# A small FFN computed on two token halves in half-width TensorE tiles

## The reference, cut to what matters

```
x = x + 0.5 * ffn(layernorm(x))
x = x + attn(layernorm(x))          # delta-rule attention, then a 512-2048-512 MLP
x = x + 0.5 * ffn(layernorm(x))

def ffn(x):                         # M = 64 units, INNER = 16 hidden values per unit
    s = einsum('btd,dm->btm', x, Win) + bin_
    h = relu(s[..., None] * W1 + b1)                 # (tokens, 64, 16)
    g = einsum('btmh,mh->btm', h, W2) + b2           # each unit's 16 values summed
    return einsum('btm,md->btd', g, Wout) + bout
```

## Time and profile before

| | |
|---|---|
| median of 3 runs | 3695.51 us (3686.24 to 3698.28) |
| the profiled execution | 3692.6 us, its span 3690.6 us |
| TensorE's mean granted clock | 0.962 of full speed |
| busy: PE, PEld | 3364.3 us (91%), 2637.4 us (71%) |
| busy: DVE, ACT, POOL | 1886.2 us (51%), 1327.8 us (36%), 1147.5 us (31%) |
| stage 1 / stage 2 / stage 3 | about 0 to 1215, 1215 to 2000, 2000 to 3691 us |

### The profile page before, as it was taken

One profiled execution on the slowest core, in us unless ns is written; L12 is line 12 of the kernel. 1 busy time (PEld: TensorE's weight loads), 2 busy tenths in 40 slices (PEclk: granted clock), 3 DMA queues, 4 the chain that ended last, 5 costly groups with the idle time before them and its releaser, 6 DMA issues. The chain is left out here.

```text
span 3690.6 us, 150931 instructions
## 1 busy us (share of the span) xinstructions
PE 3364.3 (91%) x68430; PEld 2637.4 (71%) x68430; DVE 1886.2 (51%) x3292; ACT 1327.8 (36%) x2630; POOL 1147.5 (31%) x1207
## 2 busy tenths in 40 slices
PE   3988888888896899999997899999999999999997
PEld 2666666666665688888886677777777777777775
DVE  4767766667664887877832233332333333333323
ACT  4434333344331233333333333333333333333332
POOL 0334435354452655555520112221121122122211
PEclk7999999999998899999998999999999999999998
DMA  3244353444334666665655110001000111000000
GB/s 90 81 150 121 105 159 115 115 137 133 110 122 143 196 193 192 200 192 182 187 173 167 65 35 24 23 35 35 24 35 35 35 35 35 35 30 17 35 35 23
DMA packets 388102, 355.46 MB, mean 96 GB/s; under 512 B 58128, under 2 KB 320912, under 8 KB 384912
## 3 DMA queue, kind: packets, MB, share of 16 engines
q1 hardware_dynamic: 385632, 351.27, 30.4%
q10 hardware_dynamic: 2224, 0.90, 0.1%
HBM read 184.19 MB, written 153.09 MB: 91 GB/s over the span
## 5 line engine op out<-in xcount | busy, mean ns | idle before, releaser
L1784 DVE TENSOR_TENSOR glo<-gl,gh 128x512 fp32r<-128x512 f32 x256 | 195.1, 762 | 927.3 <-ACT gh L1691 927.2
L1687 ACT ACTIVATE gl<-bank,b1m 128x512 f32<-128x512 f32 x256 | 175.9, 687 | 796.4 <-PE bank L231 796.4
L229 PE MATMUL bank<-w_hi,gh 128*128 128x512 f32 x1024 | 410.6, 401 | 24.3 <-DVE glo L1784 24.3
L229 PE MATMUL bank<-h_hi,w_hi 128*128 128x512 f32 x1024 | 425.9, 416 | 4.0 <-DVE w_lo L1828 4.0
L231 PE MATMUL bank<-w_hi,glo 128*128 128x512 f32 x1024 | 406.7, 397 | 0.0
L230 PE MATMUL bank<-h_lo,w_hi 128*128 128x512 f32 x1024 | 406.4, 397 | 0.0
L231 PE MATMUL bank<-h_hi,w_lo 128*128 128x512 f32 x1024 | 406.3, 397 | 0.0
L230 PE MATMUL bank<-w_lo,gh 128*128 128x512 f32 x1024 | 405.5, 396 | 0.0
L398 PE MATMUL bank<-qk,rawk 32*32 32x64 f32 x8192 | 166.4, 230 | 117.9 <-DVE pb L767 110.6
L398 PEld LDWEIGHTS bank<-qk,rawk 32*32 32x32 f32 x8192 | 138.4, 114 | 172.2 <-issue 170.6
L970 POOL TENSOR_TENSOR nrm<-nrm,cst 128x16 f32<-128x16 f32 x64 | 185.6, 2900 | 198.1 <-DVE nrm L738 197.8
(11 more groups left out here) (172 smaller groups left out, 7214.8 us busy)
## 6 DMA issues: line engine op xcount, KB each, us to landing
ringB<-heads_scratch SPq DMA_DIRECT2D x256, 192.0 KB, 2.7
ringA<-heads_scratch SPq DMA_DIRECT2D x258, 128.0 KB, 2.2
X<-in_L_attn_x SPq DMA_DIRECT2D x16, 1024.0 KB, 9.7
x_scratch<-X SPq DMA_DIRECT2D x16, 1024.0 KB, 5.5
heads_scratch<-vb SPq DMA_DIRECT2D x16, 1024.0 KB, 11.3
heads_scratch<-qk SPq DMA_DIRECT2D x16, 1024.0 KB, 11.0
heads_scratch<-kb SPq DMA_DIRECT2D x16, 1024.0 KB, 5.2
heads_scratch<-kbuf SPq DMA_DIRECT2D x16, 1024.0 KB, 7.7
```

The costliest lines, as they stand in the source:

```text
L229: e.matmul(o, lhs[0], rhs[0], start=first, stop=False)
L1687: e.activation(gl[k][:, :], bank[k][:, :], ACT.Gelu_apprx_tanh, bias=b1m[:, m:m + 1]).then_inc(a_gl, 1)
L1784: e.tensor_tensor(gh[k][1][:, :], gl[k][:, :], gh[k][0][:, :], ALU.subtract).then_inc(v_gl, 1)
```

## The change

The 128 partitions of the FFN's arrays hold 64 units and two halves of the inner values before; after it they hold 64 units and two halves of the tile's tokens. All 16 inner values of a unit are gathered on one partition, for 256 tokens.

- `hidden`: eight products instead of four, each of 128 rows, 64 weight columns and 256 moving columns; token half k writes partitions 64k to 64k+63 of the bank's first 256 columns, in tile position k of the array.
- `relus` and `sums`: 16 instructions of 128x256 instead of 8 of 128x512 in each; four buffers of half the size, so an activation waits for the sum four before it. Their places in the order of ACT and DVE stay, with two instructions where one was.
- `ffn_out`: four products of 64 rows instead of 128, with the blocks in the order 0, 2, 1, 3, so that neighbours use different rows of the array and different banks.
- At the start `b2t` is loaded on both halves (one DMA more, 16 instead of 15), and POOL's memset of it and the wait on that are gone; the tables `w1t`, `b1t`, `w2t` are 128x16.

The diff, cut (stage 3 is changed in the same way as stage 1):

```diff
+HALF = TOK // 2
+INNER = 16
+FFN_ORDER = (0, 2, 1, 3)
...
+    def units(pairs):
+        return [2 * q + k for q in pairs for k in range(2)]
...
-            relu1 = [sbuf(st, f"relu{i}", [P, TOK]) for i in range(2)]
-            g1 = sbuf(st, "g1", [P, TOK])
+            relu1 = sbuf(st, "relu", [P, 4, HALF])
+            g1 = sbuf(st, "g1", [P, HALF])
...
                 for f in range(NF):
-                    m = e.matmul(bank[WIN_BANK][:, :], win[:, f, :], xT1[:, f, :], start=f == 0, stop=f == NF - 1)
+                    for k in range(2):
+                        r = slice(64 * k, 64 * k + 64)
+                        m = e.matmul(bank[WIN_BANK][r, 0:HALF], win[:, f, r], xT1[:, f, k * HALF:(k + 1) * HALF],
+                                     start=f == 0, stop=f == NF - 1)
                 m.then_inc(p_win, 1)
-                released[WIN_BANK] = a_relu, 8 * t + 8
+                released[WIN_BANK] = a_relu, INNER * t + INNER
 
             def ffn_out(t):
-                e.wait_ge(v_g, 8 * t + 8)
-                for b in range(NB):
-                    bk = 6 + b % 2
+                e.wait_ge(v_g, INNER * t + INNER)
+                for n, b in enumerate(FFN_ORDER):
+                    bk, k = 6 + n % 2, b // 2
+                    r = slice(64 * k, 64 * k + 64)
                     bank_free(bk)
-                    e.matmul(bank[bk][:, :], g1[:, b * P:(b + 1) * P], wout[:, :],
+                    e.matmul(bank[bk][:, :], g1[r, b % 2 * P:(b % 2 + 1) * P], wout[r, :],
                              start=True, stop=True).then_inc(p_wout, 1)
-                    released[bk] = v_x1, 4 * t + b + 1
+                    released[bk] = v_x1, 4 * t + n + 1
...
             def relus(t, *hs):
-                for h in hs:
+                for h in units(hs):
...
-                    if 8 * t + h >= 2:
-                        e.wait_ge(v_g, 8 * t + h - 1)
-                    e.activation(relu1[h % 2][:, :], bank[WIN_BANK][:, :], ACT.Relu, bias=b1t[:, h:h + 1],
+                    if INNER * t + h >= 4:
+                        e.wait_ge(v_g, INNER * t + h - 3)
+                    e.activation(relu1[:, h % 4, :], bank[WIN_BANK][:, 0:HALF], ACT.Relu, bias=b1t[:, h:h + 1],
                                  scale=w1t[:, h:h + 1]).then_inc(a_relu, 1)
...
-            loads.append((b2t[0:64, :], col(a["L0_ffn_b2"])))
-            e.wait_ge(o_zb2, 1)
...
             def sums(t, *hs):
-                for h in hs:
-                    e.wait_ge(a_relu, 8 * t + h + 1)
+                for h in units(hs):
+                    e.wait_ge(a_relu, INNER * t + h + 1)
...
-                        e.wait_ge(v_g, 8 * t + h)
-                        e.scalar_tensor_tensor(g1[:, :], relu1[h % 2][:, :], w2t[:, h:h + 1], g1[:, :],
+                        e.wait_ge(v_g, INNER * t + h)
+                        e.scalar_tensor_tensor(g1[:, :], relu1[:, h % 4, :], w2t[:, h:h + 1], g1[:, :],
                                                ALU.mult, ALU.add).then_inc(v_g, 1)
 
             def add_ffn(t):
-                for b in range(NB):
-                    e.wait_ge(p_wout, 4 * t + b + 1)
+                for n, b in enumerate(FFN_ORDER):
+                    e.wait_ge(p_wout, 4 * t + n + 1)
                     e.wait_ge(v_xb, 4 * t + b + 1)
-                    e.tensor_tensor(X[t % 2][:, b, :], bank[6 + b % 2][:, :], X[t % 2][:, b, :],
+                    e.tensor_tensor(X[t % 2][:, b, :], bank[6 + n % 2][:, :], X[t % 2][:, b, :],
                                     ALU.add).then_inc(v_x1, 1)
...
-            e.memset(b2t[:, :], 0.0).then_inc(o_zb2, 1)
```

More of the change, by code:

```diff
@@ L129, in macaron @@
         wout = sbuf(top, "wout", [P, D])
-        w1t = sbuf(top, "w1t", [P, 8])
-        b1t = sbuf(top, "b1t", [P, 8])
-        w2t = sbuf(top, "w2t", [P, 8])
+        w1t = sbuf(top, "w1t", [P, INNER])
+        b1t = sbuf(top, "b1t", [P, INNER])
+        w2t = sbuf(top, "w2t", [P, INNER])
         bint = sbuf(top, "bint", [P, 1])
@@ L1497, in macaron @@
             ss3 = sbuf(st, "ss3", [P, NB])
-            relu3 = [sbuf(st, f"relu3{i}", [P, TOK]) for i in range(2)]
+            relu3 = sbuf(st, "relu3", [P, 4, HALF])
         stage3 = [xT3[:, f, :] for f in range(NF)] + [Z[1][:, b, :] for b in range(NB)]
@@ L1588, in hidden, with ffn_out @@
                 for f in range(NF):
-                    m = e.matmul(bank[6][:, :], win[:, f, :], xT3[:, f, :], start=f == 0, stop=f == NF - 1)
+                    for k in range(2):
+                        r = slice(64 * k, 64 * k + 64)
+                        m = e.matmul(bank[6][r, 0:HALF], win[:, f, r], xT3[:, f, k * HALF:(k + 1) * HALF],
+                                     start=f == 0, stop=f == NF - 1)
                 m.then_inc(p_win, 1)
-                released[6] = a_relu3, 8 * t + 8
-            def ffn_out(t, b):
-                bk = 6 + b % 2
-                if b == 0:
-                    e.wait_ge(v_g3, 8 * t + 8)
+                released[6] = a_relu3, INNER * t + INNER
+            def ffn_out(t, n):
+                b = FFN_ORDER[n]
+                bk, k = 6 + n % 2, b // 2
+                r = slice(64 * k, 64 * k + 64)
+                if n == 0:
+                    e.wait_ge(v_g3, INNER * t + INNER)
                 bank_free(bk)
-                e.matmul(bank[bk][:, :], g3[:, b * P:(b + 1) * P], wout[:, :],
+                e.matmul(bank[bk][:, :], g3[r, b % 2 * P:(b % 2 + 1) * P], wout[r, :],
                          start=True, stop=True).then_inc(p_wout, 1)
-                released[bk] = v_o, 4 * t + b + 1
+                released[bk] = v_o, 4 * t + n + 1
             def up(t, m):
@@ L1711, in relus @@
             def relus(t, *hs):
-                for h in hs:
+                for h in units(hs):
                     if h == 0:
                         e.wait_ge(p_win, NT + t + 1)
-                    if 8 * t + h >= 2:
-                        e.wait_ge(v_g3, 8 * t + h - 1)
-                    e.activation(relu3[h % 2][:, :], bank[6][:, :], ACT.Relu, bias=b1t[:, h:h + 1],
+                    if INNER * t + h >= 4:
+                        e.wait_ge(v_g3, INNER * t + h - 3)
+                    e.activation(relu3[:, h % 4, :], bank[6][:, 0:HALF], ACT.Relu, bias=b1t[:, h:h + 1],
                                  scale=w1t[:, h:h + 1]).then_inc(a_relu3, 1)
@@ L1808, in sums @@
             def sums(t, *hs):
-                for h in hs:
-                    e.wait_ge(a_relu3, 8 * t + h + 1)
+                for h in units(hs):
+                    e.wait_ge(a_relu3, INNER * t + h + 1)
                     if h == 0:
@@ L1813, in sums, with add_ffn @@
                             e.wait_ge(p_wout, 4 * (NT + t))
-                        e.tensor_scalar(g3[:, :], relu3[0][:, :], w2t[:, 0:1], b2t[:, 0:1],
+                        e.tensor_scalar(g3[:, :], relu3[:, 0, :], w2t[:, 0:1], b2t[:, 0:1],
                                         ALU.mult, ALU.add).then_inc(v_g3, 1)
                     else:
-                        e.wait_ge(v_g3, 8 * t + h)
-                        e.scalar_tensor_tensor(g3[:, :], relu3[h % 2][:, :], w2t[:, h:h + 1], g3[:, :],
+                        e.wait_ge(v_g3, INNER * t + h)
+                        e.scalar_tensor_tensor(g3[:, :], relu3[:, h % 4, :], w2t[:, h:h + 1], g3[:, :],
                                                ALU.mult, ALU.add).then_inc(v_g3, 1)
-            def add_ffn(t, b):
-                e.wait_ge(p_wout, 4 * (NT + t) + b + 1)
+            def add_ffn(t, n):
+                b = FFN_ORDER[n]
+                e.wait_ge(p_wout, 4 * (NT + t) + n + 1)
                 e.wait_ge(o_xb3, 4 * t + b + 1)
-                e.tensor_tensor(Z[t % 2][:, b, :], bank[6 + b % 2][:, :], Z[t % 2][:, b, :], ALU.add).then_inc(v_o, 1)
+                e.tensor_tensor(Z[t % 2][:, b, :], bank[6 + n % 2][:, :], Z[t % 2][:, b, :], ALU.add).then_inc(v_o, 1)
             def split(i):
```

12 lines of the change are left out of this document (6 added, 6 removed).

## The result

The changed kernel takes 3738.02 us (median of 4 runs, 3722.89 to 3744.1) where the kernel before took 3696.9 us beside it (3686.24 to 3702.12): the ratio is 1.0103, 95% interval 1.0083 to 1.0124. It is slower by 1.0%; the prediction was 3730 us, 0.9%. The profiled execution has a span of 3720.9 us, 30.3 more than before, and a mean granted clock of 0.949 (0.962 before). It is the fastest of the four; the medians lie 41 us apart, and the traces show where 30 of them are.

What follows compares the result with a forecast made beforehand. PE sets the pace but waits for DVE's sums in both stages. Stage 3 +9, stage 1 +17, clock +8 and start +0.6 make +35 us: 3730 us, 0.9% slower; own range 3710 to 3755, 8 in 10 from 3693 to 3772.

Steps and rivals of the forecast that it cites:

- `hidden`: On PE, two column tiles at nearly two times speed make `hidden` about 1.5 us shorter (between 0 and 1.7).
- a pair of `ffn_out`: On PE, each pair of output products gets 0.75 us shorter (between 0 and 0.85).
- a turn beside POOL: Stage 3: DVE and POOL alternate instruction by instruction, so a half-sum beside POOL takes a turn of 1.44 us.
- stall in front of `down(7)`: Stage 3, PE waiting for `gelu_low(7)`: the stall grows from 0.6 to about 2.7 us a tile.
- stage 3, a tile: Later sums against shorter `ffn_out` pairs: net +0.6 us a tile, +9 us for 15 tiles (bounds -5 and +22).
- stage 1, DVE from `bs` to the end of the long stall: Stage 1, per tile: six sums ahead of the mask +2.0 us, meetings with POOL +0.5, ReLU wait gone -1.0.
- The last tile: The FFN running alone at the end: hidden -1.5, first ReLU -0.2, eight sums +2.7, output products about -1.0: 0 us.
- The clock: Stage 1: longer stalls in front of `gram(t-1, 6)` lower PE's clock behind more of them: +8 us (0 to +12).
- Cancelled: Rival, chance 0.16: full overlap, small additions don't add, clock falls no more often: about 3698 us, within 11 of before.
- the gain arrives: Rival, chance 0.10: DVE doesn't alternate with POOL, its short sums go through in a row; stage 3 gains -57: 3665 us.
- No overlap in `hidden`: Rival, chance 0.12: the two tiles share array rows, so sixteen passes take at least 3.45 us: 3758, up to 3785.
- The clock falls in stage 3 too: Rival, chance 0.12: stalls of 2.7 and 1.5 us lower PE's clock in stage 3, 2.3 us a tile: 3765 us.

Runs made afterwards that it cites:

- split_sums: Kernel before with only ReLUs and sums split into 16 instructions of 128x256, PE's products unchanged: 3773.9 us, ratio 1.0205.
- both edits: In stage 1 DVE's masks ahead of later sums, and POOL's add_x1 after the previous tile's sums: 3639.23 us on the changed kernel, 3639.43 on the one before.
- out_twice: Changed kernel with both edits, each product of stage 1's `ffn_out` issued twice: 3636.17 us, ratio 0.9825.
- split_out: Changed kernel with both edits, stage 1's `ffn_out` in two halves with a projection between, `add_ffn` halved too: 3604.09 us, ratio 0.9734.
- late_pool: Changed kernel with POOL's add_x1 in stage 3 waiting for the sums of the tile before: 3669.32 us, ratio 0.9925.
- half_units: Changed kernel with 8 of the 16 inner values of each unit left out in both stages, PE's FFN products unchanged: 3626.57 us, ratio 0.9807.
- both_before: Kernel before the change with both edits: 3639.43 us, ratio 0.9836.
- late_pool_before: Kernel before the change with POOL's add_x1 in stage 3 waiting for the sums of the tile before: 3679.58 us, ratio 0.9944.

## Why the prediction was right

The forecast's mechanism held: the doubled sums reach PE in both stages, at POOL's additions in stage 3 and ahead of the mask in stage 1. That the total came within a few us is luck in part, since several terms were off and cancel. One by one:

| term | predicted | measured |
|---|---|---|
| spacing of half-sums alone (last tile) | 0.60 us | (8.73 - 0.49) / 14 = 0.59 |
| half-ReLU | 0.57 us | 0.565 |
| DVE busy in all | +60 us | +63.3 |
| `hidden` | -1.5 us (1.9 to 2.0 left) | -1.65 (1.95) |
| a pair of `ffn_out` | -0.75 us | 1.13 in place of 1.98, but the passes behind it only 0.65 and 0.46 sooner |
| a turn beside POOL | 1.44 us | 1.432 |
| stall in front of `down(7)` | 2.7 us | 2.30 |
| stall in front of `ffn_out`, stage 3 | near 1.5 us | 1.44 |
| `ffn_out` of stage 3 starts later by | 2.2 us | 1.52 |
| stage 3, a tile | +0.6 us | +0.60 in 11 of 14 |
| stage 1, DVE from `bs` to the end of the long stall | 2.0 + 0.5 - 1.0 = +1.5 us a tile | +1.0 |
| stage 1, wait for ReLUs | -1.0 us a tile | 22.9 to 6.5 us in all |
| stage 1, second pair of `ffn_out` | -0.3 us | -0.33 in 9 tiles |
| first tile starts | +0.6 us | +0.2 |
| the end | 0 | +0.1 |

**Stage 3.** The period of a tile, from one stall in front of `down(7)` to the next, was 101.31 us on average and is 101.91 in 11 of 14 tiles, +0.60 as forecast, but by two misses that cancel. Counted from the start of `hidden`, `gelu_low(7)` ends after 12.8 us (12.6 before; I had 13.2) and `ffn_out` starts after 17.36 (15.84 before; I had 18.0), so PE loses 1.5 us there and not 2.2. The two pairs give back 1.0 of it and not 1.5: by its rows a pair is 0.85 us shorter, but a row's duration has the pipeline's end in it. From the start of the first pair to the second pass behind it there are 1.40 us where there were 2.05, and 1.40 where there were 1.95 at the second pair, which itself starts 0.09 us later behind the pass before it; another 0.1 is lost ahead of the next `hidden`.

**The last tile** was a sum of four numbers that should cancel, and did. DVE there, without POOL:

```profile
3700.57 0.41 DVE L1829 TENSOR_SCALAR g<-relu,w2t,b2t 128x256 f32<-128x256 f32 x1 [10.04 <-ACT relu L1732]
3701.09 8.73 DVE L1833 SCALAR_TENSOR_TENSOR g<-relu,w2t,g 128x256 f32<-128x256 f32 x15
```

**Stage 1**: from the end of one tile's `turn_h` wait to the end of the long stall a tile takes 1.28 us more on average over 14 tiles (1.54 without the last one); without the clock I had 2.0 + 0.5 - 1.0 = 1.5. Over 14 tiles that is +18. But not all of it is DVE's. From `bs` on it is 1.0 us; the other 0.55 lies ahead of `bs`, where DVE waits for PE's first projections, and PE goes from `turn_h` to `hidden` at a granted clock of 0.888 instead of 0.922. split_sums shows the doubled sums' part by itself, +1.8 from `bs` on, without what the shorter `hidden` gives back.

**The clock** is where the prediction was wrong in place. I put +8 us behind the long stall, also because 2.90 us of stall had left the clock alone; the trace has a second stall of 2.90 us, which ends at 153.34, and there it fell to 0.50 from 155 to 157. Behind the long stall nothing was added: from its end to the third product of `ffn_out` there are 11.6 us in both kernels, though the stall grew by 2.3. (With both edits, where the stall grows from 2.8 to 4.2 us, the same stretch does grow, from 10.80 to 11.72 us: there the mechanism that I had in mind shows.) Instead the clock falls at `ffn_out`, in 5 of the 14 tiles, whose stretch from the third product on takes 27.9 to 29.0 us where all took 26.75 before and the other nine now take 26.4. That is 5 x 1.7 = +8.5 us, so near to my 8 by chance; the 0.55 us a tile ahead of `bs`, some 7 us in all, I had not counted. The cause at `ffn_out` is the idle time that my own gain made: shorter products end sooner, DVE frees the bank no earlier, and 1.09 us of idle time become 1.75. I had counted the gain that "goes into that stall" as nothing; it was worse than nothing. out_twice and split_out show it from two sides.

**The rivals.** *Cancelled* and *the gain arrives* fell with +30 us in the span. The second's mechanism doesn't happen, since DVE does alternate with POOL, and its condition, DVE undisturbed, was made by late_pool. The rule of the Trainium skill (SBUF — State Buffer, SBUF: two separate sides) bears on the turns: between a DVE instruction with two SBUF inputs, as these sums are, and a GpSimd instruction that reads SBUF, whichever starts first holds the shared pair of ports for its whole instruction and the other waits. The steps of 1.432 us agree with it. *No overlap in `hidden`* fell with 1.95 us. The rule behind it (the Trainium skill, TensorE: Matmul & The Clock Gate, Part 3, The mechanism: a weight load overlaps with matmuls in flight only when its row group differs) would have kept sixteen passes on the same rows apart; the measurement decides against reading it so here, at 1.95 us side by side and 2.86 in turn, both below the 3.60 of eight passes on the full array. Weight loads of the full array run beside passes as well: in the trace before, one of 0.19 us starts at 2293.16, 0.01 us behind a pass of 0.40.

*The clock falls in stage 3 too* (chance 0.12) was half right. It does fall, behind the stall in front of `down(7)` in 8 tiles and behind `ffn_out` in one. In the tile whose `hidden` starts at 3213.35, PE and then its clock:

```profile
3226.21 0.79 PE L238 MATMUL bank<-w_hi,gh 128*128 128x512 f32 x1 [2.32 <-DVE glo L1799]
...
3227.65 0.63 PE L238 MATMUL bank<-w_hi,gh 128*128 128x512 f32 x1
...
3230.73 1.13 PE L1613 MATMUL bank<-wout,g 64*128 64x512 f32 x4
```

```profile
3226.00:3230.00 4.00, 3.79 (x10) 3.03 (x11) 3.37 (x8) 3.46 (x7) 0.00 (x0) 0.57 0.00 0
3230.00:3234.00 4.00, 4.00 (x18) 2.36 (x17) 2.46 (x5) 0.15 (x1) 0.00 (x0) 1.00 0.00 0
```

The passes take 0.63 instead of 0.40 us, but what stands behind them is the same end of the sums: the stall of 1.44 us in front of `ffn_out` is gone, `ffn_out` starts 4.52 us behind `down(7)` as in the tile without a fall, and the tile is as long as its neighbours (101.88 us). Where the clock fell behind `ffn_out` (0.57 from 2516 to 2520), nothing covered it: that tile took 104.13 us. I had priced each fall at 2.3 us without asking what stands behind it; the price is right only where PE has no wait left. Two more tiles took 102.53, one with a fallen clock and one without; in these three DVE waits 0.46 us for a ReLU amid its last sums, and `ffn_out` starts 4.87 us behind `down(7)`. What the three take over 101.91 is 3.5 us together. With 14 x 0.60 that is 11.9; stage 3 rose by 10.7, since the stretch ahead of its first `hidden` is 1.6 us shorter.

Expectations of the experiments were wrong too. half_units gained 7.4 us in stage 1 where 38 were expected: the stretch that ends with the mask gave 1.8 us a tile instead of 2.5 to 3, and PE took most of that back in others, at a lower clock. both_before gained some 24 us more than I thought: 37.5 in stage 1 where I had 24, since the clock behind the long stall rose as well (11.59 us at 0.819 became 10.80 at 0.888), and 19.1 in stage 3 where I had 11. late_pool_before has 19.7 there; the two stalls that I counted are 0.76 of the 1.27 us that a tile gains, and the rest stays open.

## What to carry to other kernels

Using two halves of the array side by side does save PE's time; price what feeds and empties it, which gets twice the instructions at half the size, and beside another reader of SBUF twice the turns at the full price. Move first what collides (here one wait on POOL, 1.8% for the new form and 0.6% for the old) and then compare the forms, stage by stage: they were equal in total, and the right one in each stage was worth 1.2% more. Idle time that a shorter product leaves in front of a late partner is not neutral: look at the granted clock behind it, and at whether a wait stands behind that.

## What the hardware did that I had not expected

- Column tiles of 64 that share all 128 rows overlap for the most part: 16 passes of 256 columns in 1.95 us, against 3.60 for 8 of 512 on the whole array. On the same column tile in turn they still take only 2.86.
- The clock's fall can be bought off with useless work: each product of `ffn_out` twice, and the granted clock stays at 1.00 where it fell to 0.50, for a kernel that is no slower (3636 against 3639 us).
- A stall of 2.30 us brought the clock down behind it in some tiles of stage 3 (0.57 from 3328 to 3332) and not in others (1.00 from 2818 to 2832, behind the one that ends at 2817.97), with the same program before it.
- A fallen clock in front of a wait is free: tile periods of 101.88 to 102.05 us with it and 101.86 to 101.93 without it, the three long tiles aside.
- A row's duration overstates what shorter tiles save: pairs of `ffn_out` shrank by 0.85 us, the passes behind them came 0.65 and 0.46 us sooner. `hidden` shrank by 1.65, and from its start to `ffn_out` there are 13.28 us with late POOL, where the old form has 14.64: 1.36.
